# Weight splitting in three portions between batch 0's stages, and the values' buffer cleared behind batch 0's bias

## What is computed

```python
x = x + autocorrelation(layernorm(x), ctx, ctx)      # 8 heads, top 9 of 128 lags, softmax, gather
x = x + ffn0(layernorm(x))                           # x @ W_base.T + b_base, and a low-rank mixture
                                                     # of 8 experts (top 2), rank 16
x = x + window_attention(layernorm(x), ctx)          # 8 heads of 16 channels, window of 16
x = x + ffn1(layernorm(x))                           # a low-rank mixture of 4 experts (top 2)
```

## Time and profile before

| | us |
|---|---|
| median of 3 runs (lowest to highest) | 1823.69 (1823.42 to 1826.07) |
| the profiled execution: its own time | 1823.51 |
| the profiled execution: its span | 1821.7 |
| busy in the span: TensorE / VectorE / ScalarE / GpSimd | 1704.5 / 1571.8 / 1131.7 / 903.1 |
| share of the span: TensorE / VectorE / ScalarE / GpSimd | 94% / 86% / 62% / 50% |

### The profile page before, as it was taken

How to read it: one execution, slowest core, us unless ns; L and a number is a source line. 1 busy time by engine, 2 the same in 40 slices (tenths; PEclk the granted TensorE clock), 3 DMA queues, 4 the chain that set the end, 5 groups by cost and what they waited for, 6 DMA issues and landing times.

```text
span 1821.7 us, 48202 instructions
## 1 busy us (share of the span) xinstructions
PE 1704.5 (94%) x19296; PEld 1081.3 (59%) x19296; DVE 1571.8 (86%) x4758; ACT 1131.7 (62%) x1929; POOL 903.1 (50%) x933
## 2 busy tenths in 40 slices
PE   4699999999999999999999999999999999999975
PEld 2356566666656666655666665666665666666553
DVE  7779889889889888988988898988898998889853
ACT  5257656666765666665666676566666666657642
POOL 2355554555554545555455555444555545555432
PEclk8899999999999999999999999999999999999995
DMA  6033322243332233332223343223443322333220
GB/s 225 24 59 71 59 53 51 52 71 71 71 59 48 50 58 71 71 66 48 51 50 71 71 71 59 50 50 55 71 71 71 47 49 50 69 71 59 31 30 24
DMA packets 549359, 111.37 MB, mean 61 GB/s; under 512 B 531088, under 2 KB 531344, under 8 KB 548624
## 3 DMA queue, kind: packets, MB, share of 16 engines
q1 hardware_dynamic: 549136, 108.30, 31.8%
HBM read 57.94 MB, written 16.78 MB: 41 GB/s over the span
## 4 chain that ended last, share of the span: by engine, by line
PE 56%; DVE 20%; ACT 10%; POOL 8%; issue 5%; DMA 0%; DVEq 0%; SPq 0%; POOLq 0%; ACTq 0%
PE pb L602 18%; PE pc L677 8%; ACT q_diag L877 6%; POOL prob L1424 4%; POOL rest L1422 4%; PE pa L523 4%; ACT v_im L777 3%; PE pa L495 3%; PE pa L524 3%; PE pa L496 3%; PE pa L497 3%; PE pb L591 3%; DVE rows_c L1251 2%; PE pa L563 2%; DVE rest L1105 2%
## 5 line engine op out<-in xcount | busy, mean ns | idle before, releaser
L602 PE MATMUL pb<-w_base_h,even_words 128*128 128x512 f16 x1024 | 324.8, 379 | 0.0
L1431 POOL TENSOR_TENSOR p_hl<-sc,p_hl 128x512 f16<-128x512 f32 x128 | 164.1, 1282 | 219.9 <-ACT p_hl L777 219.9
L1458 POOL TENSOR_TENSOR sc<-sc,sc_rec 128x512 f32<-128x512 f32 x128 | 134.4, 1050 | 266.2 <-DVE sc_rec L1238 266.2
L877 ACT ACTIVATE q_diag<-sc,own 128x512 f32<-128x512 f32 x384 | 244.3, 710 | 3.1 <-DVE sc L1149 3.1
L602 PE MATMUL pb<-w_base_l,even_words 128*128 128x512 f16 x512 | 193.9, 379 | 0.0
L486 PE MATMUL pa<-xn_a,tab 128*128 128x512 f32 x384 | 180.7, 607 | 3.8 <-ACT xn_a L777 3.8
L677 PEld LDWEIGHTS pc<-sc_t,v_diag 128*128 128x128 f16 x6144 | 170.2, 97 | 20.6 <-DVE sc_t L1245 5.9
L677 PE MATMUL pc<-sc_t,v_diag 128*128 128x32 f16 x6144 | 173.9, 177 | 5.5 <-DVE sc_t L1245 5.5
L655 PE MATMUL pc<-k_h,q_diag 128*128 128x32 f16 x2048 | 169.0, 177 | 0.0
L656 PE MATMUL pc<-k_l,q_diag 128*128 128x32 f16 x2048 | 168.4, 177 | 0.0
L657 PE MATMUL pc<-k_h,q_diag 128*128 128x32 f16 x2048 | 168.4, 177 | 0.0
(11 more groups left out here) (165 smaller groups left out, 4658.4 us busy)
## 6 DMA issues: line engine op xcount, KB each, us to landing
x_a<-in_x SPq DMA_DIRECT2D x32, 512.0 KB, 5.8
x_res<-in_ctx_in SPq DMA_DIRECT2D x32, 512.0 KB, 5.6
x_res<-in_x SPq DMA_DIRECT2D x32, 512.0 KB, 3.7
v_diag<-even_words SPq DMA_DIRECT2D x128, 128.0 KB, 4.9
v_diag<-p_hl SPq DMA_DIRECT2D x128, 128.0 KB, 5.0
out<-rows_c SPq DMA_DIRECT2D x32, 512.0 KB, 2.6
v_diag<-in_base_w SPq DMA_DIRECT2D x4, 1024.0 KB, 10.1
q_diag<-in_ra SPq DMA_DIRECT2D x1, 544.0 KB, 13.8
```

What stands on the lines that cost most here:

```text
L602: mm(pb[:, h, :], rows[:, cols], weights[:, j, h * HALF:(h + 1) * HALF], start=(j == 0 and m == 0), stop=False)
L877: nc.scalar.activation(q_diag[:, blocks, head * QB:(head + 1) * QB], q_hl.rearrange("p (n t) -> p n t", t=QB)[:, blocks], ACT.Copy, scale= ...
L1431: g_.tensor_tensor(part[:, :, :, LO], sc[:, g % 2, :, :], part[:, :, :, HI], ALU.subtract)\
L1458: g_.tensor_tensor(sc[:, g % 2, :, :], sc[:, g % 2, :, :], sc_rec[:, blocks].unsqueeze(2).to_broadcast([P, GB, KEYS]), ALU.mult)\
```

## The change

ScalarE makes the high part of the first base quarter earlier, between the two `a_values_long` of batch 0. Quarters 2 to 4 and `ra0` stay behind `a_exp`; `b0` and `b1` come behind `a_transposed`. VectorE makes the four low parts of the base weights where it made all seven, and those of `ra0`, `b0` and `b1` behind `a_products`, ahead of `a_residual`. On GpSimd `clear_values` and `b_bias` of batch 0 change places. Transfers and TensorE's order are the same.

```diff
--- before.py
+++ after.py
@@ -917,17 +917,19 @@
                 act.wait_ge(tr_x[1].sem, tr_x[1].after(b, h + 1))
                 copy(xt_c[:, h * HALF:(h + 1) * HALF], pc[:, h, :]).then_inc(xt_out[1].sem, 1)
 
-            def split_weights():
+            def split_weights(parts):
                 flat_h = w_base_h[:, :, :].rearrange("p k n -> p (k n)")
-                act.wait_ge(w_in.sem, 16 * (SPLITS + 4))
-                for part in range(SPLITS):
-                    cols = slice(part * KT * D // SPLITS, (part + 1) * KT * D // SPLITS)
-                    nc.scalar.activation(flat_h[:, cols], base_f32[:, cols], ACT.Copy, scale=W_SCALE)\
-                        .then_inc(w_hi.sem, 1)
-                nc.scalar.activation(w_ra0_h[:, :, :].rearrange("p k n -> p (k n)"), ra0_f32, ACT.Copy,
-                                     scale=W_SCALE).then_inc(w_hi.sem, 1)
-                for part, whole in ((w_b0_h, b0_f32), (w_b1_hh, b1_f32)):
-                    nc.scalar.activation(part[:, :], whole, ACT.Copy, scale=W_SCALE).then_inc(w_hi.sem, 1)
+                for part in parts:
+                    quarter = min(part, SPLITS - 1)
+                    cols = slice(quarter * KT * D // SPLITS, (quarter + 1) * KT * D // SPLITS)
+                    high, whole = [
+                        (flat_h[:, cols], base_f32[:, cols]),
+                        (w_ra0_h[:, :, :].rearrange("p k n -> p (k n)"), ra0_f32),
+                        (w_b0_h[:, :], b0_f32),
+                        (w_b1_hh[:, :], b1_f32)][max(0, part - SPLITS + 1)]
+                    if part == 0:
+                        act.wait_ge(w_in.sem, 16 * (SPLITS + 4))
+                    nc.scalar.activation(high, whole, ACT.Copy, scale=W_SCALE).then_inc(w_hi.sem, 1)
 
             def step(i, live):
                 if live(3):
@@ -941,6 +943,9 @@
                     c_exp(i - 3, 1)
                 if live(1):
                     a_values_long(i - 1, 0)
+                if first(i - 1):
+                    split_weights(range(1))
+                if live(1):
                     a_values_long(i - 1, 1)
                 if live(3):
                     c_high(i - 3, 1)
@@ -959,7 +964,7 @@
                 if live(1):
                     a_exp(i - 1, 1)
                 if first(i - 1):
-                    split_weights()
+                    split_weights(range(1, SPLITS + 1))
                 if live(3):
                     c_attended(i - 3, 1)
                     c_high(i - 3, 3)
@@ -973,6 +978,8 @@
                 if live(1):
                     a_transposed(i - 1, 0)
                     a_transposed(i - 1, 1)
+                if first(i - 1):
+                    split_weights(range(SPLITS + 1, WEIGHTS_SPLIT))
                 if live(2):
                     spread(i - 2, 2, x_c, xn_b)
                 if live(3):
@@ -1303,7 +1310,7 @@
                 if live(0):
                     a_softmax(i)
                 if first(i - 0):
-                    split_weights(range(WEIGHTS_SPLIT))
+                    split_weights(range(SPLITS))
                 if live(1):
                     b_values_low(i - 1)
                 if live(-1):
@@ -1328,6 +1335,8 @@
                 if live(0):
                     a_products(i, 2)
                     a_products(i, 3)
+                if first(i):
+                    split_weights(range(SPLITS, WEIGHTS_SPLIT))
                 if live(1):
                     b_values(i - 1, 1)
                     b_queries(i - 1)
@@ -1468,10 +1477,10 @@
                     b_query_blocks(i - 1, 7, 1)
                 if live(0):
                     root(i, 1)
-                if first(i - 0):
+                if live(0):
+                    b_bias(i)
+                if first(i):
                     clear_values()
-                if live(0):
-                    b_bias(i)
                 if live(1):
                     c_normalise(i - 1, 0)
                     c_low(i - 1, 0)
```

More of the change, by code:

```diff
@@ L1470, in step @@
                     root(i, 1)
-                if first(i - 0):
-                    clear_values()
                 if live(0):
                     b_bias(i)
+                if first(i):
+                    clear_values()
                 if live(1):
```

## The result

The changed kernel takes 1814.53 us (median of 6 runs, 1813.17 to 1817.54), the kernel before 1824.28 us in the runs taken beside it (6 runs, 1823.42 to 1826.07). The ratio is 0.9947, with a 95% interval of 0.9934 to 0.996: 9.75 us less. The forecast was 1815.4, from 1812.4 to 1818.4.

What follows compares the result with a forecast made beforehand. The prediction took the first 80 us, a chain of waits up to TensorE's first router, to decide the time, the loop's rhythm staying. -0.5 (edit 1) - 6.07 - 1.63 = -8.2 gave 1815.4 us, range 1812.4 to 1818.4.

Steps and rivals of the forecast that it cites:

- The frame: Whole kernel: the loop's 53.74 us period stays, so only the first 80 us, up to the first router, matter.
- Rivals 4 and 5: Batch 1's start: an unseen path sets it, 1823.6 us, chance 0.03; loop: settles in another, slower rhythm, chance 0.03.
- The stall: VectorE's L1038 of batch 0 no longer waits for GpSimd's memset, so the correlations start sooner: -6.07 us.
- Rival 3: The stall only moves: the memset also holds VectorE's work beside it; 1819.4 us, chance 0.08.
- The clock in the correlations behind `x_b`: First half of TensorE's correlations runs at full instead of half clock: -1.63 us, bounds 0 and 1.63.
- rival 2: TensorE's clock stays at half in the first correlations; 1817.0 us, chance 0.17.
- The turns: Three VectorE low parts and GpSimd's four sums alternate, each waiting for the other; some 2.2 us paid back.
- Rival 1: Low parts and sums hardly disturb each other, or GpSimd goes first; 1813.2 to 1814.5 us, chance 0.19.
- -3.47: VectorE: three low parts leave the chain ahead of the products, saving 3.47 us.
- The early quarter: ScalarE's first high part ahead of batch 0's exponentials makes the softmax start later: +0.75 us.
- the landing: Arrival of the last weight, which ScalarE's first quarter needs, taken as 24.6 us.
- The later landing's 1.35: If the last weight landed 0.6 us later, the softmax would start +1.35 us later instead of +0.75.

Runs made afterwards that it cites:

- edit 2: The part of the change that puts GpSimd's clear_values behind b_bias of batch 0; alone against the kernel before 1819.25 us.
- e5: Kernel before plus 26 matmuls with unused results on TensorE during the stall, ahead of the transposes of xn_b; 1823.06 us (one run).
- e8: e4 with matmuls of unused results added in TensorE's idle stretches; 1808.15 us.
- e9: Kernel before with edit 2 alone, plus matmuls of unused results in TensorE's idle stretches; 1808.92 us.
- e4: Changed kernel with the low parts of b0 and b1 moved just ahead of the next softmax; 1813.98 us.
- e7: Changed kernel plus matmuls of unused results in TensorE's idle stretches; 1809.07 us.
- e10: Kernel before with edit 1 alone, plus matmuls of unused results in TensorE's idle stretches; 1816.76 us.
- e6: Kernel before plus matmuls of unused results in TensorE's idle stretches, nothing else changed; 1814.90 us.
- edit 1: The part of the change that splits the weights in portions on ScalarE and VectorE; alone against the kernel before 1826.60 us.
- e2: Changed kernel with clear_values back ahead of b_bias, so edit 1 alone; 1826.60 us.
- e3: Changed kernel with all seven of ScalarE's high parts behind a_exp again; 1815.00 us.
- e1: Kernel before with edit 2 alone, the weights' splitting as before; 1819.25 us.
- e11: Changed kernel with added matmuls, low parts and statistics placed apart from GpSimd's sums and normalisation, ScalarE's high parts all behind a_exp; 1803.47 us.

## Why the prediction was right, and where it was not

**The frame held.** The period stayed 53.74 us, and router 1 to router 29 is the same within 0.2 us everywhere. Rivals 4 and 5 fell with it. That only the first 80 us matter held for what the change moves, and not for the time (below).

**The stall, -6.07**: -6.00, in after, and within 0.01 of it in all eight experiments that have edit 2. L1045 at 0.81 us beside no memset, and L1067 then waiting for ScalarE's `v_im` (0.48 us): the next thing late was named rightly. Rival 3 fell: VectorE's lines beside the memset kept their lengths.

**The clock in the correlations behind `x_b`, -1.63**: -1.52 in after, and e5 shows the same 1.52 with the stall left in place. It doesn't always come: in e8 and e9 the correlations ran at half the clock although the stall was gone, and 1.6 us with them, which is rival 2 in another kernel.

**The turns**: forecast 8.47 us from the first sum's start (48.83) to the last one's end (57.3), measured 7.95; first sum to `x_b` 2.18 us longer, where "some 2.2" was forecast. The price was right on both engines (2.28 for a low part beside a sum), and e4 took two turns away and got two short sums back. Rival 1 fell by these rows. The time alone would not have told: 1814.53 lies nearer to rival 1's 1814.5 than to the forecast's 1815.4. Softmax to `x_b` follows: -3.47 + 2.2 = -1.27 forecast, -1.28 measured.

**The early quarter, +0.75**: this term was mis-sized. In after's trace it doesn't show, because TensorE's half clock from 19.8 us made `v_im` late anyway. With the clock kept, exponentials came 2.4 and 2.9 us later (e7, e10 against e6), the softmax 1.4 and 1.9. Some 0.4 of each is a shift that `v_re` (21.55 and 21.61 against 21.17) shows already, so the term is 1.0 and 1.4. The step that failed is the landing: taken as 24.6 from one trace, it was 24.98 in e7 and later still in e10, where the quarter starts at 25.47. The later landing's 1.35 stood in the prediction as the other end. So edit 1 as a whole is not -0.5 but between +1.9 and 0 with the clock kept.

**What the sum left out.** 8.2 forecast, 9.75 measured, and the traces' parts don't agree with the forecast's as well as the total does. The router came 5.77 us sooner and not 8.2 (the softmax was 3.02 later), and 1.9 came from two stretches that the prediction didn't mention, between router 0 and 1 and behind router 29. In both the instructions are the same. In the first the granted clock is not (0.88 before and 1.00 after, from 96 to 110 us). In the second the half-clock stretches add up to 50 us in either kernel and only fall at other places, and I can't say why it is 1.17 us shorter. Both shorter lengths stand in e5 as well, which has neither edit. So part of the right total is luck. With the clock kept at both kernels the change is worth 5.8 us, about 6.0 of it edit 2.

**What stays open.** Why the clock falls in one kernel's correlations and not in another's. The early half stretch is in after, e2, e3, e4 and e5 and not in before and e1, but TensorE's instructions up to there are the same in all seven, e5 has neither edit, and there is one trace of each. Nor is it shown, only argued from the two columns and the clock shares of the runs, that all of the 4.7 us between e1 and after is the clock.

## What to carry to other kernels

Before moving an instruction into one engine's idle time, look at what the engine that excludes it does there: VectorE's gap was GpSimd's busiest moment, and 3.5 us of low parts came back as 3 us of turns, while beside a memset (two SBUF inputs) or with statistics beside GpSimd's normalisation nobody stood still. Don't put work whose input lands late ahead of work that is ready sooner, even into an idle moment: here that cost 1.0 and 1.4 us. And compare versions with TensorE's idle stretches filled alike, or the clock's level in stretches that the change doesn't touch is read as its effect.

## What the runs showed of the hardware

**Turns.** When VectorE and GpSimd both had instructions with two inputs in SBUF queued, neither ran two in a row: 1.27, then 2.31, 2.24, 2.24 on GpSimd, 1.45, 2.28, 2.28 on VectorE. Each waited for the one instruction of the other. e2, e7 and e10 show the same lengths within 0.01 us.

**Length doesn't matter.** In e11 a GpSimd instruction on 128 x 1 elements, 0.19 us elsewhere, took 2.23 (L1452), behind a low part of 2.2 us.

**The clock as the larger prize.** Filling TensorE's idle stretches alone made the kernel before 10.2 us faster by the medians (1825.07 to 1814.90). Between the traces it is 9.0: 5.6 us of that lie behind router 29 (190.44 to 184.89), 1.6 between softmax and `x_b`, 0.9 between `x_b` and router and 0.7 between router 0 and 1. The added matmuls cost nothing that shows. The last row of after's stretches (1760 to 1812 us) shows what is to be had there: a granted clock of 0.57. In e7 the same stretch has 0.88:

```profile
1760.00:1812.00 52.00, 33.56 (x483) 19.98 (x481) 20.00 (x58) 18.67 (x36) 14.09 (x14) 0.88 0.14 31
```
